# A fixed home for x's transposed tiles in a graph-attention block: seven copies on VectorE per batch instead of two alternating halves

## What is computed

```python
qkv = (x @ w_qkv).reshape(b, n, 3, H, hd).transpose(2, 0, 3, 1, 4)      # H = 8 heads of hd = 64
q, k, v = (qkv[0], qkv[1], qkv[2])
attn = jnp.einsum('bhnd,bhmd->bhnm', q, k) * scale
attn = jnp.where(attn_mask[None, None] == 0, -jnp.inf, attn)            # attn_mask = adj
attn = jax.nn.softmax(attn, axis=-1)
o = jnp.einsum('bhnm,bhmd->bhnd', attn, v).transpose(0, 2, 1, 3).reshape(b, n, d)
o = o @ w_proj + b_proj
...
ln = (o - mu) * jax.lax.rsqrt(var + LN_EPS) * ln_gamma + ln_beta
out = layernorm(x + o + ln)
```

## Time and profile before

| | |
|---|---|
| median of 3 runs | 3244.41 us (3243.56 to 3247.23) |
| the profiled execution | 3245.11 us, its span 3243.0 us |
| granted TensorE clock, mean | 0.989 of full speed |
| PE busy, share of the span | 3097.0 us, 95% |
| ACT | 2625.4 us, 81% |
| POOL | 2489.8 us, 77% |
| DVE | 2353.4 us, 73% |
| transposing DMAs' queue q1, share of 16 engines | 92.1% |

### The profile page before, as it was taken

The page is one execution under the profiler, slowest core; times in us unless marked ns, Lnnn a source line. Parts: engine busy times, 40 slices in busy tenths (PEclk is TensorE's granted clock), DMA queues, the critical chain, the costliest instruction groups (busy, mean ns, idle before and its releaser), DMA issues.

```text
span 3243.0 us, 124702 instructions
## 1 busy us (share of the span) xinstructions
PE 3097.0 (95%) x42504; PEld 1909.2 (59%) x42504; DVE 2353.4 (73%) x4496; ACT 2625.4 (81%) x3849; POOL 2489.8 (77%) x1543
## 2 busy tenths in 40 slices
PE   6899999999999999999999999999999999999984
PEld 3555655656656656656656656656656566556552
DVE  5657777777777777777777777777777777777765
ACT  5887888888888888888888888888888888888881
POOL 3777787787787787787787777877777777878783
PEclk9999999999999999999999999999999999999996
DMA  8999999999999999999999999999999999999994
GB/s 216 186 196 202 198 207 205 198 209 205 196 207 205 201 204 204 203 203 204 203 205 201 205 204 202 205 204 200 205 206 198 206 205 197 207 205 200 195 200 90
DMA packets 2187077, 648.04 MB, mean 200 GB/s; under 512 B 2135408, under 2 KB 2135408, under 8 KB 2186992
## 3 DMA queue, kind: packets, MB, share of 16 engines
q1 hardware_dynamic: 2133808, 548.28, 92.1%
q10 hardware_dynamic: 53184, 98.59, 9.5%
HBM read 76.28 MB, written 33.55 MB: 34 GB/s over the span
## 4 chain that ended last, share of the span: by engine, by line
PE 80%; SPq 10%; issue 3%; DMA 2%; DVE 2%; POOL 1%; ACT 1%; DVEq 0%; ACTq 0%; POOLq 0%
PE scores_a L387 19%; PE side L351 18%; PE side L337 12%; SPq L289 10%; PE proj L368 9%; PE pv_bank L408 7%; PE pv_bank L410 6%; PE pv_bank L409 6%; DMA pt<-p_split 2%; PE side L332 2%; PE side L328 2%; POOL p_split L743 1%; ACT p L480 0%; ACT p_split L493 0%; PE scores_b L387 0%
## 5 line engine op out<-in xcount | busy, mean ns | idle before, releaser
L743 POOL TENSOR_TENSOR p_split<-p,p_split 128x1024 f16<-128x1024 f32 x1024 | 2170.9, 2139 | 680.6 <-ACT p_split L493 680.1
L480 ACT ACTIVATE p<-p,row_min 128x1024 f32<-128x1024 f32 x1024 | 1171.8, 1145 | 280.9 <-DVE row_min L628 280.7
L493 ACT ACTIVATE p_split<-p 128x1024 f16<-128x1024 f32 x1024 | 1049.2, 1047 | 102.0 <-DMA pt<-p_split 101.5
L628 DVE CUSTOM_DVE_ANT_0 p<-scores_a,mask_q 128x1024 f32<-128x1024 f32 x512 | 626.9, 1224 | 362.7 <-PE scores_b L387 308.5
L408 PE MATMUL pv_bank<-v_both,pt 128*128 128x64 f16 x8192 | 827.0, 193 | 45.2 <-DMA pt<-p_split 32.9
L410 PE MATMUL pv_bank<-v_both,pt 128*128 128x64 f16 x8192 | 828.2, 193 | 0.0
L409 PE MATMUL pv_bank<-v_both,pt 128*128 128x64 f16 x8192 | 827.9, 193 | 0.0
L408 PEld LDWEIGHTS pv_bank<-v_both,pt 128*128 128x128 f16 x8192 | 737.8, 98 | 134.1 <-issue 67.3
L409 PEld LDWEIGHTS pv_bank<-v_both,pt 128*128 128x128 f16 x8192 | 728.2, 98 | 73.2
L410 PEld LDWEIGHTS pv_bank<-v_both,pt 128*128 128x128 f16 x8192 | 729.2, 98 | 0.0
L351 PE MATMUL side<-xt,w_hi 128*128 (+1 forms) x2048 | 633.9, 381 | 13.4 <-DVE q_lo L617 6.0
(11 more groups left out here) (79 smaller groups left out, 4286.9 us busy)
## 6 DMA issues: line engine op xcount, KB each, us to landing
x_in<-in_x ACTq DMA_DIRECT2D x60, 512.0 KB, 5.2
x_res<-in_x ACTq DMA_DIRECT2D x120, 256.0 KB, 3.7
out<-x_res ACTq DMA_DIRECT2D x120, 256.0 KB, 4.2
pt<-p_split SPq DMA_TRANSPOSE x1024, 4.9
pt<-in_adj SPq DMA_DIRECT2D x8, 512.0 KB, 8.9
ot<-in_L_gnn_w_qkv SPq DMA_DIRECT2D x4, 768.0 KB, 9.0
p<-in_x SPq DMA_DIRECT2D x8, 256.0 KB, 5.0
p<-in_x ACTq DMA_DIRECT2D x8, 256.0 KB, 9.5
```

Source lines behind the costliest of these rows:

```text
L480: nc.scalar.activation(p32[:, slot, :], p32[:, slot, :], ACT.Exp, bias=row_min[:, slot:slot + 1], scale=-1.0, accum_out=row_sum[:, head:he ...
L493: nc.scalar.activation(p_split[:, head % RING, HI, :], p32[:, head % RING, :], ACT.Copy).then_inc(hi_done, 1)
L628: nc.vector.tensor_tensor_reduce(out=p32[:, slot, :], in0=scores[ab][:, :], in1=mask_q[:, u, :], scale=-SCALE, scalar=3.0e38, op0=ALU.add, ...
L743: nc.gpsimd.tensor_tensor(p_split[:, slot, LO, :], p32[:, slot, :], p_split[:, slot, HI, :], ALU.subtract).then_inc(lo_done, 1)
```

## The change

`xt` becomes `[P, 2 * T - 1, 2, KC, P]`: 15 places for tiles instead of 16. The tiles of the batch in work always lie at home, places 11 to 14 (tiles 0 to 3) and 0 to 3 (tiles 4 to 7). X0 and X1 write the next batch's tiles to waiting places, 7 to 10 (X0) and 6 down to 3 (X1); the last of these, place 3, is tile 7's home. In the last body of a batch, once V1 has been computed, VectorE copies the other seven tiles home, one `tensor_copy` of 128 x 1024 fp16 each, in the slots of `COPY`. In the loop each copy stands under a test of its own, `(g & 3) == 3`. Two semaphores `x_copied` tell PE: Q0 waits for the first four copies, K1 for all seven and for X1, for which Q0 waited before. V0 and V1 are taken by VectorE at slot 12 instead of 10 and 11, X1 at 18 instead of 15, and one step of the second layer norm moves from slot 34 to 36. VectorE's waits for ScalarE's takes are instructions of their own now. `COST` and `ORDER` are adjusted.

```diff
@@
-ORDER = [("Q1", 0, 12), ("X0", 0, 4), ("V0", 0, 48), ("V1", 0, 48), ("P0", 0, 4), ("O1", 0, 4), ("P0", 4, 7),
+ORDER = [("Q1", 0, 12), ("X0", 0, 4), ("V0", 0, 48), ("V1", 0, 48), ("P0", 0, 3), ("O1", 0, 4), ("P0", 3, 7),
...
-COST = {"Q": 9, "V": 2.5, "O": 4, "K": 10, "P": 9, "X": 5}
+COST = {"Q": 8, "V": 2.5, "O": 4, "K": 10, "P": 9, "X": 8}
...
-TAKE_DVE = {"Q1": 4, "X0": 5, "V0": 10, "V1": 11, "O1": 14, "X1": 15, "Q0": 22, "K0": 29, "K1": 30, "O0": 30}
-LOAD_X = 18
+TAKE_DVE = {"Q1": 4, "X0": 5, "V0": 12, "V1": 12, "O1": 14, "X1": 18, "Q0": 22, "K0": 29, "K1": 30, "O0": 30}
+
+COPY = [12, 13, 13, 15, 16, 17, 17]
+LOAD_X = 20
...
-        xt = sb("xt", [P, 2, T, 2, KC, P], F16)
+        xt = sb("xt", [P, 2 * T - 1, 2, KC, P], F16)
...
+        x_copied = sems("x_copied", 2)
...
+        def at_end(eng, g, do):
+
+            if not known(g):
+                with eng.If((g & 3) == 3):
+                    do()
+            elif (g + 1) % PAIRS == 0 and 0 < batch(g + 1) < B:
+                do()
+
+        def place(t):
+            return t - 4 if t >= 4 else t + 11
+
+        def waiting(g, i):
+
+            return 6 - pair(g) if i else pair(g) + 7
...
-                    mm = nc.tensor.matmul(bank[:, c * P:(c + 1) * P], xt[:, parity(batch(g)), t, rows, k, :],
+                    mm = nc.tensor.matmul(bank[:, c * P:(c + 1) * P], xt[:, place(t), rows, k, :],
...
-                    if i == 0 and kind == NEXT_FIRST and active(g, "X1"):
+                    if i == 0 and kind == "K1" and active(g, "X1"):
                         wait_alone(pe, side_dve, side_done(g, "X1"))
+                    if i == 0 and kind == NEXT_FIRST:
+                        wait_alone(pe, x_copied[0], batch(g + 1))
+                    if i == 0 and kind == "K1":
+                        wait_alone(pe, x_copied[1], batch(g + 1))
...
-                                          xt[:, parity(batch(of)), 4 * half:4 * half + 4, x_half, k, :],
+                                          xt[:, place(4 * half):place(4 * half) + 4, x_half, k, :],
...
-                wait(dve, side_act, side_done(g, kind))
+                wait_alone(dve, side_act, side_done(g, kind))
...
+            def copy_tile(g, t):
+
+                if t == 0:
+                    wait_alone(dve, side_ready, side_done(g, "V1"))
+                    wait_alone(dve, side_dve, side_done(g, "X0"))
+                move = nc.vector.tensor_copy(xt[:, place(t), :, :, :].rearrange("p h k n -> p (h k n)"),
+                                             xt[:, waiting(t // 2, t % 2), :, :, :].rearrange("p h k n -> p (h k n)"))
+                if t in (3, 6):
+                    move.then_inc(x_copied[t // 4], 1)
...
+                    for t in range(7):
+                        if COPY[t] == s:
+                            at_end(dve, g, lambda: copy_tile(g, t))
```

More of the change, by code:

```diff
@@ L465, in take @@
                 elif kind[0] == "X":
-                    nc.scalar.activation(xt[:, parity(batch(g + PAIRS)), pair(g) * 2 + half, HI, :, :],
+                    nc.scalar.activation(xt[:, waiting(g, half), HI, :, :],
                                          bank[:, :].rearrange("p (k n) -> p k n", k=KC), ACT.Copy).then_inc(side_act, 1)
@@ L606, in take @@
                 elif kind[0] == "X":
-                    at, tile = parity(batch(g + PAIRS)), pair(g) * 2 + half
-                    nc.vector.tensor_tensor(xt[:, at, tile, LO, :, :], bank[:, :].rearrange("p (k n) -> p k n", k=KC),
-                                            xt[:, at, tile, HI, :, :], ALU.subtract).then_inc(side_dve, 1)
+                    tile = waiting(g, half)
+                    nc.vector.tensor_tensor(xt[:, tile, LO, :, :], bank[:, :].rearrange("p (k n) -> p k n", k=KC),
+                                            xt[:, tile, HI, :, :], ALU.subtract).then_inc(side_dve, 1)
                 elif kind[0] == "V":
```

8 lines of the change are left out of this document (4 added, 4 removed).

## The result

The changed kernel takes 3216.07 us (median of four runs, 3214.41 to 3217.14), the kernel before 3245.13 us beside it (3243.56 to 3247.23): a ratio of 0.991, 95% interval 0.9892 to 0.9927. It is 29 us faster where 103 were forecast, and lies above the range. The profiled execution took 3214.41 us with a span of 3212.6.

The account below looks back on a forecast made before the run. PE's sequencer in two of eight units was the bound. 54 loop bodies x (48.98 - 46.6) = 128.5 us, less 21 for copies and 5 for loop entry, gave 102.5 off 3245.11: 3142 us, range 3105 to 3200.

Parts of the forecast that it names:

- What bounds the kernel: Loop body, V's matmuls: TensorE's queue computes operand addresses and starves the array in units 1 and 2; at least 2.66 us.
- the 46.07 of the sum: Least time of a loop body in us: 48.98 less 1.65 (unit 1), 1.01 (unit 2) and 0.25 (unit 4).
- Unit 2: Late V matmuls and P0's preparation: 1.01 us gained a body, or 0.55 if the hole before P0 stays.
- Unit 1: First V matmuls: fewer register instructions gain 1.65 us a body, with 0.3 us kept as doubt.
- coupling with the DMAs: Loop body: 0.5 us added to TensorE's 46.07 for the transposing DMAs and the thinner slack of the minima.
- Unit 4: Start of Q0: it no longer waits for X1, gaining 0.25 us in three bodies of four.
- The rival that they bound the loop at 47.9: Transposing DMAs become the bound at once, 47.9 us a loop body, 3191 us in all; chance 0.19.
- Tests and new waits: VectorE: seven tests a body, 2.1 us (0.4 to 4.1), fit into idle time; ten waits as instructions cost nothing.
- The copies: Last body of a batch, units 3 and 4: seven VectorE copies of 0.69 us each cost 1.5 us a body.
- the upper bound of 4 us: Most that the copies could cost a last body, taken from copies of 1.22 us, the minimum's duration.
- The rival that was right: VectorE copies and POOL operations exclude each other: 3.1 us a copy, 12 us a last body, 3289 us; chance 0.05.
- the average case: Same exclusion, but each copy finds on average 0.8 us of a POOL operation ahead: 5.8 us a body, 3198 at most.

Follow-up runs that it names:

- last run: Changed kernel with copies in slots 12, 12, 12, 12, 14, 18, 22, and X0 put ahead of Q1 so V0 reuses X0's bank: 3108.85 us, ratio 0.9584.

## Why the prediction was wrong

- **What bounds the kernel: right.** TensorE's sequencer did hold the loop back, and the loop body without its stalls is 46.28 us (last run), 0.2 above the 46.07 of the sum and 0.04 below the written-out body 59.
- **Unit 2: right in size.** Forecast 1.01, measured 6.81 - 5.86 = 0.95 us.
- **Unit 1: mis-sized, the smaller cause of the miss.** The step was "I take the whole 1.65, and keep 0.3 us as doubt". It gave 0.95, of which some 0.1 is X0's fourth transpose that went to unit 0 (5.83 to 5.97 us). The argument that the queue enters V "behind 1.4 us of score matmuls" was wrong: it stood in the wait for Q1's low part until 1498.26, when the scores were nearly through. Fixing V's addresses gave the missing 0.7 back, and moving the wait gave it back too. Over 54 bodies that is 38 us in the step. The 0.5 us a body that was kept for coupling with the DMAs covered most of it, by luck.
- **Unit 4: half.** Q0's wait for X1 did go, but units 3 and 4 together fell from 11.97 to 11.87 us (body 10), 0.10 and not 0.25. The rest stands ahead of Q0 again: in its new place behind P.V, whose 24 matmuls take 0.70 us from 2.06 us into the unit, it starts at 2.91 and not 2.76. What fills these 0.15 us was not tried.
- **The coupling with the DMAs: not there.** The body runs at 46.28 us with the same transposes, at 215 GB/s. The rival that they bound the loop at 47.9 fell; the 0.5 us covered another error.
- **Tests and new waits: right as far as is shown.** Unit 3, in whose time three of the tests fall, takes 5.57 us in the loop of the kernel without copies, and 5.57 in body 59 of the last run, written out without any test. Unit 4, with the other four, takes 6.27 against 6.14; but the same two bodies were 0.25 us apart before there were any tests (6.18 and 5.93).
- **The copies: the step that failed.** "So 1.5 us for each last body" was built on a duration, 0.69 us, that no copy has: it is 0.42 alone and up to 2.38 beside GpSimd. The slack was right to 0.14 us. The runs showed waits for GpSimd in its place: 4.6 us of kernel time in each of 15 bodies (4.9 in body 11). So the upper bound of 4 us was too low, because it came from the duration of another operation and not from a wait for another engine.
- **The rival that was right, and how I talked it down.** It was given 0.05 at 3289 us, and the average case, "0.8 in all seven", 3198 at most. The average itself came out: over all 105 copies the time above 0.42 us is 0.88 us a copy, 6.1 a body. What was wrong is the step from there to TensorE, "of which idle time hides a part", with 4 us as its most. The waits are not spread evenly. GpSimd's low part starts 0.88 to 0.91 us behind the start of unit 3's first minimum in every last body of the loop (591.77 and 592.68 in body 11), so a copy behind that minimum finds an operation some 0.24 us old, and a second one behind it finds the next. Three of the seven copies waited for nearly a whole operation each and in about half of the bodies a fourth in part, all of them between the two minima of a unit, ahead of the one that TensorE's next scores wait for: that made 3.07 us in unit 3 and 1.86 in unit 4. The rival was right in its mechanism and not in its size: its 12 us a body charged a whole wait to all seven copies.
- **The clock: left out, at almost no cost.** The forecast had TensorE standing for 1.0 us; at 3.00 the granted clock fell as well in 11 of 15 bodies. In nine of these the time was hidden behind the late minimum; in two it cost 0.9 us each.
- **Two slips in the sum.** It takes 14 last bodies where 15 have copies, and Q0's 0.25 us in all 54 bodies though it was argued for 41 of them. Together that is 5 us. Its lower bound for a copy was no bound either: 0.18 us is not VectorE's smallest operation (one on a single column takes 0.15).

The balance against the forecast, by the spans of the two profiled executions, which differ by 30 us where 102 were forecast: 41 ordinary loop bodies at 47.1 in place of 46.6, 20 us; 13 last ones at 52.0 in place of 48.1, 51 us; bodies 3 and 59, which grew by 6.1 (from 45.3) and 5.2 where the sum had 1.5 for one of them, 10 us. That is 81 us of the 72 that are missing. Of the other 9, 4 are the entry of the loop, which cost 1 us more than before where 5 were kept; 5 were gained outside the loop, mostly in body 60 and behind it, which I did not follow up.

## What to carry to other kernels

Where VectorE gets a copy from SBUF to SBUF, look in the trace at what GpSimd does at that very place. Its share of busy time gave the mean wait well here, and not what the waits cost: engines that follow each other through semaphores meet at the same phase each time, and the same seven copies cost 69 us in one set of slots and 4 to 7 in others. Never put two such copies in a row where GpSimd has work queued. Leave one alone inside a known slack, and count that slack for each unit (here 0.93 to 1.98 us), put several where GpSimd is idle, or use a slower form that is not held up, as the multiplication with a sum was here. Instructions of a sequencer cost by where they stand: behind a wait that passes late eight cost 0.7 us a body here, and moving the wait was worth as much as removing them. And before a fallen clock is charged, look at what ends the stretch: where it is another engine, the clock costs nothing.

## What the runs showed of the hardware

- A VectorE copy of 128x1024 two-byte elements takes 0.42 us alone and 2.15 to 2.38 us when it meets the start of GpSimd's tensor operation of 2.14 (less behind one that has run for a while: 1.15, 1.27, 1.77 us); GpSimd's operation in turn grows to 2.30 to 2.35 us. A copy of 64 elements (0.17 us) waits behind a running one in the same way (1.90 us), but a second small one slips through ahead of GpSimd's next. What decides who goes first was not tried.
- A 32-bit OR with two inputs in SBUF, 0.68 us alone, takes 2.27 to 2.62 us there. A multiplication with a sum, one input, 1.21 us, is unaffected, and so are the minima, 1.22 us everywhere, with one input in SBUF and one in PSUM.
- After 3.0 us or more without a matmul the granted clock fell to 1.2 GHz in most cases (11 of 15 last bodies of the changed kernel, 14 of 15 with no copies between unit 4's minima), but not in all: body 59 kept it after 3.4 us. Where TensorE's own pace set the time of unit 4, that cost 1.4 us in most bodies, 2.7 in four and none in one; where VectorE set it, nothing in most. With matmuls in the gap it did not fall in any of 14.
- Three tests with jumps in VectorE's queue cost no measurable time in unit 3 (5.57 us with and without them).
- Eight register operations on TensorE's queue (46 and 32 ns each) cost 0.7 us a body behind a wait passed 1.45 us into the unit, and none of that when it was passed at 0.52 to 0.68.
